# Reordering VectorE's work in the expert steps of a graph and mixture-of-experts kernel: result adds ahead of the second matrix' low part, and the last step's second matrix made ready earlier

## Chip, cores and metric

The kernel runs on one core of a Trainium2 chip. The metric is device time in microseconds; three runs of the kernel before have a median of 1210.55 us.

## What is computed

Two GraphSAGE layers and then a mixture of experts, all in float32, on 1250 rows of 1024 features. Only the expert part is touched:

```python
t = layernorm(x)                                   # [1250, 1024]
logits = silu(t @ rw1 + rb1) @ rw2 + rb2           # 8 experts
vals, idx = top_k(logits, 2); w = softmax over the two
eh = silu(einsum('td,edh->teh', t, ew1) + eb1)     # hidden 256
eo = einsum('teh,ehd->ted', eh, ew2) + eb2
y = t + einsum('te,ted->td', w, eo)
out = x + y
```

## The kernel before

The router sorts the 2 x 1250 (row, expert) pairs by expert into blocks, and 17 **expert steps** (NS) of 256 rows (M) go through them, each with one expert's two matrices: ew1 (1024 x 256, 1 MB) and ew2 (256 x 1024, 1 MB). Everything that is multiplied is split in two parts of reduced precision: a high part that ScalarE writes as a copy, and a low part, which is what VectorE gets by subtracting the high part from the raw value. Each product is then three matmuls (high x high, high x low, low x high). The step number is s; u is the buffer (s % 2), every tile has two; b counts the step's two halves of 128 rows.

Each engine has its own written order, and semaphores join them. `pipeline(e, n, (lag, part), ...)` (line 70) runs through t = 0, 1, ..., and in each t calls each part with s = t - lag, in the order of the list; `skewed` (line 86) is the pair (0, head), (1, tail).

- **SP** (lines 1892 to 1906) loads the raw matrices, w1 and w2 of step s, 1 MB each. Each load waits until VectorE has made the low part of step s - 2 of the same matrix (m_wlo, which is given 2 at the start), since the raw buffer is free then.
- **TensorE** (1939 to 1989), step t: the first product of step t in two halves of 24 matmuls (L1969), each followed by 8 transposes of the gathered rows of step t + 1 (L1955), then the second product of step t - 1, 4 groups of 6 matmuls (L1985), one for each 128 rows x 512 columns.
- **ScalarE** (1997 to 2043), step t: `shift(t - 1)` writes bias times router weight into o_rows (L2035), which waits for m_kept; then `head(t)`: SiLU of the first product (L2021), the high part of the transposed rows of step t + 1 (L2015), of the hidden values (L2026), of the first matrix of step t + 1 (`w1`, L2005), and of the second matrix of step t (`w2`, L2010).
- **VectorE** (2045 to 2083), step t: the low part of the transposed rows of step t + 1 (L2056, 4 groups), of the hidden values of step t (L2062), of the first matrix of step t + 1 and of the second matrix of step t (both L2051); then `tail(t - 1)`: 4 adds of the second product, times the router weight, into o_rows (L2073). The first two adds complete half b = 0, the other two b = 1; each raises m_out.
- **GpSimd** (1908 to 1937) issues the indirect DMAs. `scatter(s)` (L1921) adds the 256 finished rows of o_rows to `out` in memory, in two halves. As rows may repeat between steps, it first waits until both halves of the scatter of step s - 1 have landed (m_st); only then does it raise m_kept, which releases ScalarE's `shift(s + 1)`; each half then waits for its two adds. The gather of 256 rows (L1928), in two halves as well, reads the inputs of a later step.

Of the kernel before, what the change touches and what calls it, by code (L numbers as in the profile page):

```python
# [62 lines left out]
NS = (TOP * N + NX * (M - 1)) // M  # L63
# [6 lines left out]
def pipeline(e, n, *stages):  # L70


    deepest = max(lag for lag, _ in stages)
    for t in range(n + deepest):
        for lag, part in stages:
            if 0 <= t - lag < n:
                part(t - lag, (t - lag) % 2, (t - lag) // 2)
# [8 lines left out]
def skewed(e, n, head, tail):  # L86

    pipeline(e, n, (0, head), (1, tail))


def build(nc, I, out):
    ctx = ExitStack()
    with ctx:
        prog = {k: [] for k in ("sync", "scalar", "vector", "gpsimd", "tensor")}

        def on(engine):

            return prog[engine].append
# [216 lines left out]
        w2_raw = S("w2_raw", [128, 2, HK, D], F32)  # L315
        w2_hi = S("w2_hi", [128, 2, HK, D], F32R)
        w2_lo = S("w2_lo", [128, 2, HK, D], F32R)
# [27 lines left out]
        def wait_apart(e, sem, value):  # L345


            e.wait_ge(sem, value)
            e.sem_inc(s_none, 1)

        @on("gpsimd")
        def _(e):
            e.memset(zero[:], 0.0).then_inc(s_id, 1)
            e.memset(ident[:], 0.0).then_inc(s_id, 1)
            e.wait_ge(s_id, 2)
            e.affine_select(out=ident[:], in_=ident[:], compare_op=ALU.not_equal, fill=1.0, base=0,
                            pattern=[[-1, 128]], channel_multiplier=1).then_inc(s_id, 1)
            e.memset(ones[:], 1.0).then_inc(s_ones, 1)
            e.memset(epst[:], EPS).then_inc(s_ones, 1)
# [371 lines left out]
        def four(engine, table, s, top_):  # L731

            _, values = nc.values_load_multi_w_load_instructions(table[0:1, s:s + 4], engines=[engine], min_val=0, max_val=top_)
            return values
# [1150 lines left out]
        def gated(e):  # L1885

            e.wait_ge(g_x, 1)
            base_stored(e)
            for u in range(2):
                e.wait_ge(t_st[u], 32 * (NT // 2))  # L1890
# [100 lines left out]
        def more(s):  # L1991
            return not isinstance(s, int) or s < NS - 1
# [4 lines left out]
        @on("scalar")  # L1997
        def _(e):
            gated(e)
            e.wait_ge(g_eb, 32)  # L2000

            def w1(s, u, q):
                e.wait_ge(m_win[0][u], 16 * q + 16)
                e.wait_ge(m_g1, HK * s + HK)
                e.activation(w1_hi[:, u], w1_raw[:, u], ACT.Copy).then_inc(m_whi[0], 1)  # L2005

            def w2(s, u, q):
                e.wait_ge(m_win[1][u], 16 * q + 16)
                e.wait_ge(m_g2, NB * s + NB)
                e.activation(w2_hi[:, u], w2_raw[:, u], ACT.Copy).then_inc(m_whi[1], 1)  # L2010

            def rows(s, u, q, groups=range(4)):
                for g in groups:
                    e.wait_ge(m_tx, 4 * s + g + 1 + 8)
                    e.activation(group(xt_hi, u, g), bank(g), ACT.Copy).then_inc(m_xhi, 1)  # L2015

            def head(s, u, q):
                x = e.value_load(step_x[0:1, ds(s, 1)], min_val=0, max_val=NX - 1)
                for j in range(HK):
                    wait_apart(e, m_g1, HK * s + j + 1 + 4)  # L2020
                    e.activation(hid[:, u, j, :], ps[:, 2 + j, 0:M], ACT.Silu, bias=eb1c[:, ds(x * HK + j, 1)]).then_inc(m_h, 1)  # L2021
                    if more(s):
                        rows(s + 1, 1 - u, q + u, range(2 * j, 2 * j + 2))
                e.wait_ge(m_h, HK * s + HK + 2)
                e.wait_ge(m_g2, NB * s + NB)
                e.activation(hid_hi[:, u], hid[:, u], ACT.Copy).then_inc(m_hhi, 1)  # L2026
                if more(s):
                    w1(s + 1, 1 - u, q + u)
                w2(s, u, q)

            def shift(s, u, q):
                x = e.value_load(step_x[0:1, ds(s, 1)], min_val=0, max_val=NX - 1)
                e.wait_ge(m_kept, s + 1)
                for b in range(SUB):
                    e.activation(o_rows[:, u, b, :], eb2_all[:, ds(x, 1), :].rearrange("p a n -> p (a n)"), ACT.Copy,  # L2035
                                 scale=slot_w[:, ds(s * SUB + b, 1)]).then_inc(m_eb, 1)

            e.sem_inc(m_out, 2 * NB)
            w1(0, 0, 0)
            rows(0, 0, 0)  # L2040
            e.wait_ge(g_to, 2)
            e.wait_ge(g_b2, 16)
            pipeline(e, NS, (1, shift), (0, head))

        @on("vector")
        def _(e):
            gated(e)

            def w(i, raw, hi, lo, s, u, q):
                e.wait_ge(m_whi[i], s + 1)  # L2050
                e.tensor_tensor(lo[:, u], raw[:, u], hi[:, u].bitcast(F32), ALU.subtract).then_inc(m_wlo[i], 1)  # L2051

            def rows(s, u, q, groups=range(4)):
                for g in groups:
                    e.wait_ge(m_xhi, 4 * s + g + 1)
                    e.tensor_tensor(group(xt_lo, u, g), bank(g), group(xt_hi, u, g).bitcast(F32), ALU.subtract).then_inc(m_xlo, 1)  # L2056

            def head(s, u, q):
                if more(s):
                    rows(s + 1, 1 - u, q + u)  # L2060
                e.wait_ge(m_hhi, s + 1)
                e.tensor_tensor(hid_lo[:, u], hid[:, u], hid_hi[:, u].bitcast(F32), ALU.subtract).then_inc(m_hlo, 1)  # L2062
                if more(s):
                    w(0, w1_raw, w1_hi, w1_lo, s + 1, 1 - u, q + u)
                w(1, w2_raw, w2_hi, w2_lo, s, u, q)

            def tail(s, u, q):
                for b in range(SUB):
                    e.wait_ge(m_eb, SUB * s + b + 1)
                    for half in range(2):  # L2070
                        e.wait_ge(m_g2, NB * s + 2 * b + half + 1 + 2 * NB)
                        cols = o_rows[:, u, b, 512 * half:512 * half + 512]
                        e.scalar_tensor_tensor(out=cols, in0=ps[:, 4 + 2 * b + half, :], scalar=slot_w[:, ds(s * SUB + b, 1)],  # L2073
                                               in1=cols, op0=ALU.mult, op1=ALU.add).then_inc(m_out, 1)
            w(0, w1_raw, w1_hi, w1_lo, 0, 0, 0)
            rows(0, 0, 0)
            e.wait_ge(g_pe, 5)
            e.tensor_copy(parts3[:], ps[:, 6, 0:3 * NB_]).then_inc(g_sl, 1)
            e.wait_ge(g_sl, 1)
            e.tensor_tensor(slot_w[:], parts3[:, 2 * NB_:3 * NB_], parts3[:, NB_:2 * NB_], ALU.add).then_inc(g_sl, 1)  # L2080
            e.wait_ge(g_sl, 2)
            e.tensor_tensor(slot_w[:], slot_w[:], parts3[:, 0:NB_], ALU.add).then_inc(g_to, 1)
            skewed(e, NS, head, tail)


        @on("sync")
# [39 lines left out]
```

## Time and profile before

| what | value |
|---|---|
| median of 3 runs | 1210.55 us (1208.05 to 1214.05) |
| profiled execution, own time | 1209.29 us |
| its span, first to last instruction | 1207.6 us |
| TensorE busy | 1099.3 us, 91% of the span |
| VectorE busy | 641.2 us, 53% |
| ScalarE busy | 459.7 us, 38% |
| moved by DMA | 160.18 MB, mean 133 GB/s |
| the 17 expert steps | from about 940 us to the end |

The times of instructions below are microseconds from the start of the span. The matmul ends are modelled, and descriptors and transfers of a DMA are not part of the instruction that issues it: the row of a DMA_INDIRECT is the time in which GpSimd writes its descriptors. A wait is shown in brackets behind a row, as the idle time of the engine before it and what ended that.

### The profile page before, as it was taken

To read this page: it belongs to the slowest core of one execution; us is meant where nothing else is said; L and a number is where in the kernel's file an instruction comes from. 1 tells how busy PE (TensorE), PEld (TensorE's weight loads), DVE (VectorE), ACT (ScalarE), POOL (GpSimd) and SP (SyncE) were. 2 spreads that over 40 slices of the span, in tenths; PEclk is the share of its full clock that TensorE was granted. 3 is DMA by queue.
4 is the path that set the end of the run, shared out by engine and by line. 5 is a ranking of instruction groups with operands and counts; after the bars stand their busy time and mean duration, and the time that the engine had idled before them with its cause. 6 is when DMAs were issued, how large, how long until landed. Compare 5 with 4: busy or idle time off the path is not lost.

```text
span 1207.6 us, 19102 instructions
## 1 busy us (share of the span) xinstructions
PE 1099.3 (91%) x6584; PEld 1026.7 (85%) x6584; DVE 641.2 (53%) x1112; ACT 459.7 (38%) x939; POOL 158.5 (13%) x178
## 2 busy tenths in 40 slices
PE   2698999999998999999999999999994799999992
PEld 1697888888888999999999999999993698888882
DVE  5737777777836243225223522642225477777772
ACT  5643434343511222111112011552332566766770
POOL 2000000000000002000200200014421133333322
PEclk9999999999999999999999999999997699999997
DMA  5411331133123752014102400765541779999975
GB/s 132 130 38 62 100 94 51 56 100 100 45 85 102 225 159 58 1 28 141 46 1 102 136 1 1 221 201 157 182 179 60 288 248 309 294 300 297 307 178 90
DMA packets 74817, 160.18 MB, mean 133 GB/s; under 512 B 11135, under 2 KB 49980, under 8 KB 70226
## 3 DMA queue, kind: packets, MB, share of 16 engines
q1 hardware_dynamic: 61117, 112.34, 29.6%
q0 software_dynamic: 12992, 45.90, 14.7%
q8 instruction: 68, 1.11, 0.4%
q10 hardware_dynamic: 596, 0.48, 0.1%
q14 instruction: 44, 0.35, 0.1%
HBM read 112.07 MB, written 46.63 MB: 131 GB/s over the span
## 4 chain that ended last, share of the span: by engine, by line
PE 55%; DMA 5%; DVE 5%; issue 2%; ACT 2%; POOL 0%; ACTq 0%; SPq 0%; POOLq 0%; DVEq 0%; PEld 0%
PE ps L1366 19%; PE ps L1438 9%; PE ps L1405 7%; PE ps L1097 7%; PE ps L1969 5%; DMA out<-o_rows,to_i 4%; PE ps L1985 4%; DVE w_lo L2051 2%; PE ps L1955 2%; PE ps L854 1%; ACT w_hi L2005 1%; DVE o_rows L2073 1%; DMA self_part<-self_d 1%; PE ps L1424 1%; ACT o_rows L2035 1%
## 5 line engine op out<-in xcount | busy, mean ns | idle before, releaser
L729 DVE TENSOR_TENSOR adj<-ps,adj 125x250 f32 x212 | 87.7, 414 | 65.5 <-issue 30.6
L854 PE MATMUL ps<-h_lo,w_hi 128*128 128x418 f32 x336 | 109.2, 372 | 0.0
L1328 POOL TENSOR_TENSOR s_rows<-s_rows,b1t 125x1368 f32<-125x1368 f32 (+3 forms) x9 | 23.6, 2633 | 644.8 <-DMA s_rows<-in_x 644.8
L854 PE MATMUL ps<-h_hi,w_hi 128*128 128x418 f32 x336 | 100.4, 380 | 0.0
L722 PE MATMUL ps<-key_hot,src_hot 125*125 125x250 bf16 x424 | 81.9, 274 | 16.3 <-DVE adj L729 13.1
L1405 PE MATMUL ps<-z_hi,adj 125*125 125x342 f32 (+1 forms) x300 | 95.1, 322 | 1.3 <-DVE s_rows L1637 1.3
L1405 PE MATMUL ps<-z_lo,adj 125*125 125x342 f32 (+1 forms) x300 | 94.3, 319 | 1.4 <-issue 1.4
L854 PE MATMUL ps<-h_hi,w_lo 128*128 128x418 f32 x336 | 93.5, 359 | 0.0
L1097 PE MATMUL ps<-adj,y_hi 125*128 125x416 f32 (+1 forms) x240 | 85.6, 357 | 4.1 <-issue 3.4
L722 PEld LDWEIGHTS ps<-key_hot,src_hot 125*125 125x125 bf16 x424 | 51.8, 136 | 44.0 <-issue 22.6
L1969 PE MATMUL ps<-xt_hi,w_hi 128*128 128x256 f32 x272 | 81.9, 301 | 7.0 <-DVE w_lo L2051 5.5
L2051 DVE TENSOR_TENSOR w_lo<-w_raw,w_hi 128x2048 fp32r<-128x2048 f32 x34 | 76.5, 2289 | 20.2 <-ACT w_hi L2005 19.0
L1097 PE MATMUL ps<-adj,y_lo 125*128 125x416 f32 (+1 forms) x240 | 85.4, 356 | 0.4 <-issue 0.4
L1969 PE MATMUL ps<-xt_lo,w_hi 128*128 128x256 f32 x272 | 78.7, 289 | 0.0
L1969 PE MATMUL ps<-xt_hi,w_lo 128*128 128x256 f32 x272 | 78.6, 289 | 0.0
L1366 PE MATMUL ps<-wn_hi,hs_lo 128*125 128x342 f32 (+1 forms) x240 | 76.7, 320 | 0.0
L1366 PE MATMUL ps<-wn_hi,hs_hi 128*125 128x342 f32 (+1 forms) x240 | 76.7, 320 | 0.0
L1366 PE MATMUL ps<-ws_hi,hs_hi 128*125 128x342 f32 (+1 forms) x240 | 76.7, 320 | 0.0
L1366 PE MATMUL ps<-ws_lo,hs_hi 128*125 128x342 f32 (+1 forms) x240 | 76.7, 319 | 0.0
L1366 PE MATMUL ps<-ws_hi,hs_lo 128*125 128x342 f32 (+1 forms) x240 | 76.6, 319 | 0.0
L1366 PE MATMUL ps<-wn_lo,hs_hi 128*125 128x342 f32 (+1 forms) x240 | 76.5, 319 | 0.0
L704 ACT ACTIVATE src_now<-scol 125x4 f16 x212 | 41.3, 195 | 92.0 <-DVE key_hot L715 76.7
(282 smaller groups left out, 2767.9 us busy)
## 6 DMA issues: line engine op xcount, KB each, us to landing
w_raw<-in_L_ffn_ew SPq DMA_DIRECT2D x34, 1024.0 KB
xin<-in_x SPq DMA_DIRECT2D x10, 448.0 KB
t_d<-xn SPq DMA_DIRECT2D x10, 448.0 KB
base<-x_d POOLq DMA_DIRECT2D x10, 448.0 KB, 4.2
out<-base POOLq DMA_DIRECT2D x10, 448.0 KB, 3.5
y_d<-y_hi SPq DMA_DIRECT2D x7, 625.0 KB
y_d<-y_lo SPq DMA_DIRECT2D x7, 625.0 KB
self_d<-self SPq DMA_DIRECT2D x7, 625.0 KB
```

The costliest lines, as they stand in the source:

```text
L704: e.activation(src_now[:, b, :, :], twice(scol), ACT.Copy)
L722: mm = e.matmul(ps[0:P, 5 + b % 2, 0:KW], src_hot[:, b, g, 0:P], key_hot[:, b, g, :], start=(g == 0), stop=(g == G - 1))
L729: e.tensor_tensor(cols, ps[0:P, 5 + b % 2, 0:KW].rearrange("p (t w) -> p t w", t=NT), cols, ALU.add).then_inc(self.took, 1)
L854: mm = e.matmul(BANK(m, own, c), wt[:, own, k, :], ht[:, k, a:a + w], start=(k == 0 and p == 0), stop=(k == KT - 1 and p == 2))
L1097: mm = e.matmul(ps[:, banks[c], 0:w], y[:, k, :], adj_[:, k, a:a + w], start=(n == 1), stop=(n == 2 * NT))
L1366: mm = e.matmul(ps[0:P, 2 * v + u, 0:w], ht[:, u, k, :], wt[v][:, k, 0:w], start=(k == EARLY[0] and p == 0), stop=(k == LATE_K[-1] and p = ...
L1405: mm = e.matmul(ps[0:P, 2 + n % 2, 0:w], adj_[:, k, tile_of(j)], z[:, k, 0:w], start=(k == 0 and p == 0), stop=(k == NT - 1 and p == 1))
L1438: mm = e.matmul(ps[:, i % 5, 0:w], wt[u][:, k, :], ht[:, k, a:a + w], start=(n == 1), stop=(n == 3 * KT))
L1955: mm = e.transpose(ps[:, g % 2, k * M + 128 * b:k * M + 128 * b + 128], x_rows[:, u, b, 128 * (2 * g + k):128 * (2 * g + k + 1)], ident[:])
L1969: mm = e.matmul(ps[:, 2 + j, 0:M], wt[:, u, k, 128 * j:128 * j + 128], xt[:, u, k, :], start=(n == 1), stop=(n == 3 * KT))
L1985: mm = e.matmul(ps[:, 4 + 2 * b + half, :], ht[:, u, j, 128 * b:128 * b + 128], wt[:, u, j, 512 * half:512 * half + 512], start=(n == 1), ...
L2051: e.tensor_tensor(lo[:, u], raw[:, u], hi[:, u].bitcast(F32), ALU.subtract).then_inc(m_wlo[i], 1)
```

## The change

VectorE's step keeps the same instructions in another order: the 4 adds of step t - 1 come ahead of the low part of the second matrix of step t. In the last step the low part of the second matrix is made first of all, ahead of the hidden values' low part. ScalarE writes the last step's high part of the second matrix at the start of that step, ahead of `shift` and `head`, rather than at its end.

```diff
@@ -2026,9 +2026,11 @@
                 e.activation(hid_hi[:, u], hid[:, u], ACT.Copy).then_inc(m_hhi, 1)
                 if more(s):
                     w1(s + 1, 1 - u, q + u)
-                w2(s, u, q)
+                    w2(s, u, q)
 
             def shift(s, u, q):
+                if s == NS - 2:
+                    w2(s + 1, 1 - u, q + u)
                 x = e.value_load(step_x[0:1, ds(s, 1)], min_val=0, max_val=NX - 1)
                 e.wait_ge(m_kept, s + 1)
                 for b in range(SUB):
@@ -2058,11 +2060,16 @@
             def head(s, u, q):
                 if more(s):
                     rows(s + 1, 1 - u, q + u)
+                else:
+                    w(1, w2_raw, w2_hi, w2_lo, s, u, q)
                 e.wait_ge(m_hhi, s + 1)
                 e.tensor_tensor(hid_lo[:, u], hid[:, u], hid_hi[:, u].bitcast(F32), ALU.subtract).then_inc(m_hlo, 1)
                 if more(s):
                     w(0, w1_raw, w1_hi, w1_lo, s + 1, 1 - u, q + u)
-                w(1, w2_raw, w2_hi, w2_lo, s, u, q)
+
+            def second(s, u, q):
+                if more(s):
+                    w(1, w2_raw, w2_hi, w2_lo, s, u, q)
 
             def tail(s, u, q):
                 for b in range(SUB):
@@ -2080,7 +2087,7 @@
             e.tensor_tensor(slot_w[:], parts3[:, 2 * NB_:3 * NB_], parts3[:, NB_:2 * NB_], ALU.add).then_inc(g_sl, 1)
             e.wait_ge(g_sl, 2)
             e.tensor_tensor(slot_w[:], slot_w[:], parts3[:, 0:NB_], ALU.add).then_inc(g_to, 1)
-            skewed(e, NS, head, tail)
+            pipeline(e, NS, (0, head), (1, tail), (0, second))
 
 
         @on("sync")
```

## Rows read from the trace of the kernel before

**Rows 1.** Windows before and with scatters: PE, PEld, DVE, ACT, POOL, PEclk, DMA, GB/s.
```profile
971.00:984.00 13.00, 13.00 (x89) 11.72 (x88) 9.96 (x12) 8.85 (x12) 5.03 (x4) 1.00 0.63 219
...
1060.00:1080.00 20.00, 19.15 (x134) 17.16 (x133) 13.83 (x18) 14.04 (x19) 8.33 (x6) 1.00 1.02 327
```

**Rows 2.** Waits, 960 to 1208 us: total, times, longest.
```profile
ACT o_rows L2035 <- POOLq L1918: 57.3, 15, 5.3
```

**Rows 3.** VectorE timeline: start, length, instruction, idle before.
```profile
973.22 4.49 DVE L2051 TENSOR_TENSOR w_lo<-w_raw,w_hi 128x2048 fp32r<-128x2048 f32 x2 [0.93 <-ACT w_hi L2005]
...
1054.92 4.50 DVE L2051 TENSOR_TENSOR w_lo<-w_raw,w_hi 128x2048 fp32r<-128x2048 f32 x2 [1.04 <-ACT w_hi L2005]
1059.33 2.72 DVE L2073 SCALAR_TENSOR_TENSOR o_rows<-ps,slot_w,o_rows 128x512 f32<-128x512 f32 x4
...
1069.08 4.49 DVE L2051 TENSOR_TENSOR w_lo<-w_raw,w_hi 128x2048 fp32r<-128x2048 f32 x2 [1.03 <-ACT w_hi L2005]
...
1082.74 4.49 DVE L2051 TENSOR_TENSOR w_lo<-w_raw,w_hi 128x2048 fp32r<-128x2048 f32 x2 [1.03 <-ACT w_hi L2005]
...
1097.87 4.50 DVE L2051 TENSOR_TENSOR w_lo<-w_raw,w_hi 128x2048 fp32r<-128x2048 f32 x2 [1.04 <-ACT w_hi L2005]
...
1111.12 4.49 DVE L2051 TENSOR_TENSOR w_lo<-w_raw,w_hi 128x2048 fp32r<-128x2048 f32 x2 [0.93 <-ACT w_hi L2005]
```

**Rows 4.** ScalarE timeline: preparing the output rows.
```profile
991.83 2.19 ACT L2035 ACTIVATE o_rows<-eb_all,slot_w 128x1024 f32 x2 [3.60 <-POOLq L1918]
...
1061.02 2.19 ACT L2035 ACTIVATE o_rows<-eb_all,slot_w 128x1024 f32 x2 [4.33 <-POOLq L1918]
...
1074.67 2.19 ACT L2035 ACTIVATE o_rows<-eb_all,slot_w 128x1024 f32 x2 [3.81 <-POOLq L1918]
...
1089.81 2.19 ACT L2035 ACTIVATE o_rows<-eb_all,slot_w 128x1024 f32 x2 [5.30 <-POOLq L1918]
...
1102.89 2.19 ACT L2035 ACTIVATE o_rows<-eb_all,slot_w 128x1024 f32 x2 [3.25 <-POOLq L1918]
...
1157.92 2.19 ACT L2035 ACTIVATE o_rows<-eb_all,slot_w 128x1024 f32 x2 [3.66 <-POOLq L1918]
```

**Rows 5.** GpSimd timeline: issues of the scatter's first half.
```profile
979.92 1.65 POOL L1921 DMA_INDIRECT out<-o_rows,to_i  x1 [6.81 <-DVE o_rows L2073]
...
1061.78 1.61 POOL L1921 DMA_INDIRECT out<-o_rows,to_i  x1 [6.74 <-DVE o_rows L2073]
...
1145.49 1.61 POOL L1921 DMA_INDIRECT out<-o_rows,to_i  x1 [6.54 <-DVE o_rows L2073]
```

**Rows 6.** DMA queues, 1008.2 to 1011.9 us: packets, MB, share of 16 engines.
```profile
q1 hardware_dynamic: 186, 1.40, 97.5%
q0 software_dynamic: 9, 0.03, 2.8%
```

**Rows 7.** VectorE timeline, the end.
```profile
1165.98 4.49 DVE L2051 TENSOR_TENSOR w_lo<-w_raw,w_hi 128x2048 fp32r<-128x2048 f32 x2 [1.03 <-ACT w_hi L2005]
1170.39 2.72 DVE L2073 SCALAR_TENSOR_TENSOR o_rows<-ps,slot_w,o_rows 128x512 f32<-128x512 f32 x4
...
1177.53 2.29 DVE L2051 TENSOR_TENSOR w_lo<-w_raw,w_hi 128x2048 fp32r<-128x2048 f32 x1 [1.11 <-ACT w_hi L2010]
1179.74 2.72 DVE L2073 SCALAR_TENSOR_TENSOR o_rows<-ps,slot_w,o_rows 128x512 f32<-128x512 f32 x4
```

**Rows 8.** GpSimd timeline, the end.
```profile
1172.59 1.56 POOL L1921 DMA_INDIRECT out<-o_rows,to_i  x1 [10.06 <-DVE o_rows L2073]
...
1183.00 1.58 POOL L1921 DMA_INDIRECT out<-o_rows,to_i  x1 [6.99 <-DVE o_rows L2073]
...
1192.62 1.56 POOL L1921 DMA_INDIRECT out<-o_rows,to_i  x1 [6.17 <-DMA out<-o_rows,to_i]
```

**Rows 9.** ScalarE timeline, the end.
```profile
1175.59 1.90 ACT L2010 ACTIVATE w_hi<-w_raw 128x2048 fp32r<-128x2048 f32 x1
1181.85 2.20 ACT L2035 ACTIVATE o_rows<-eb_all,slot_w 128x1024 f32 x2 [4.35 <-POOLq L1918]
```

## The prediction

> **What bounds the kernel now.** Only the 17 expert steps change, so I read views of that stage alone. First the windows [rows 1]: with scatters running, TensorE is busy 19.15 of 20 us at full granted clock, VectorE 13.83, ScalarE 14.04, and the DMA engines are occupied all the time (share 1.02, 327 GB/s), against 0.63 before scatters begin. TensorE is the engine to fill; the DMA share is the warning. Next the waits [rows 2]: the largest that a busy engine has is ScalarE's, 57.3 us in 15 waits for GpSimd's line 1918. That line releases `shift` once the scatter before has landed. ScalarE works in order, so SiLU and the high part of the next rows are queued behind `shift`, VectorE's low part behind these, and TensorE's transposes behind that. A late landing thus becomes a gap on TensorE.
>
> How late is too late stands in the timelines. Let W be the start of a step's pair of w_lo subtractions (the beat), O the start of `shift` in the next beat. From W to the next W [rows 3], with O - W [rows 4]:
> - O 5.02 after 1097.87: next beat in 13.25 us
> - 5.59 after 1069.08: 13.66
> - 6.10 after 1054.92: 14.16
> - 7.07 after 1082.74: 15.13
>
> That is a line: step = 13.25 + (O - W - 5.18), and never under 13.25. So 13.25 us is what TensorE needs by itself. From the W at 973.22 to the one at 1165.98 [rows 3, 7] are 14 steps in 192.76 us, 13.77 each; 14 x 13.25 is 185.5. **The late landings cost 7.3 us.**
>
> Why is O late? The adds start 4.41 after W, behind both subtractions (1059.33 against 1054.92) [rows 3]. The scatter is issued once two adds are done and the previous one has landed: where adds decide, 6.6 after W (1172.59 - 1165.98) [rows 7, 8]; where the landing decides, 0.76 after O (1061.78 against 1061.02) [rows 4, 5]. From the first half's issue to O (the latency D) is 11.91 us for the first (979.92 to 991.83) and 12.43 for the 13th (1145.49 to 1157.92) [rows 4, 5]; the 13 between them average 12.71. The loop closes: O comes 6.6 + 12.7 = 19.3 after the W before it, hence 19.3 - step after its own, and step = 13.25 + 19.3 - step - 5.18 gives 13.7, close to the 13.77 seen.
>
> **The change, part by part.**
>
> *Adds ahead of the second subtraction, steps 1 to 15.* Nothing is added or removed; the 4 adds start 2.2 us earlier (half the pair of 4.49), the second subtraction 2.72 later, the length of the adds [rows 3]. Their inputs are there: `shift` for them ran in the previous beat, and TensorE's last group of the second product ends near the start of the second subtraction, so at most the fourth add waits, a fraction of its 0.7 us. Adds-gated issues now stand 4.4 after W. With D unchanged, O is 17.1 after W, 3.9 after the next: 1.3 inside the 5.18. The other gate now bites: scatters can't follow each other in under D + 0.76 = 13.47 us. O drifts 0.22 us a step against 13.25, uses up the 1.3 in 6 steps, and the 7 or so left cost 0.22 each, 1.6 us. D is not even, and long ones can't be won back by short ones: the average loop gives 13.71 where 13.77 came out, so I take another 0.7 us over the steps. Gain: 7.3 - 1.6 - 0.7 = **5.0 us**.
>
> D is the one unknown. Nothing in the trace shows a scatter asked for ahead of the weights. Before, SP asks for the two raw matrices at the end of the pair, 2.2 us ahead of the first half's issue, and while they move the scatter's queue gets 2.8% of the engines against 97.5% [rows 6]. Afterwards that request comes at W + 7.1 (4.41 + 2.72), 2.7 behind the first half's issue and just behind the second's, as the first takes GpSimd 1.6 [rows 5]. Lower bound: no weights in the way, 9.26 (1172.59 to 1181.85) [rows 8, 9]; then all 7.3 us are won. Upper bound: the whole pair cuts in between the halves, 2 MB at the 1.40 MB in 3.7 us of [rows 6], 5.4 us more: 14.7. I keep 12.7, the nearest rows, which are of the same loaded stage; below it the result hardly moves.
>
> For two requests at once the Trainium skill (DMA: Bandwidth & Descriptors, Queues, rings and completion order) says that each DMA engine takes turns between queues, packet by packet. By that rule the weights would slow the second half but not hold it, and D would lie between my bounds; rows 6 show no such turns within that stretch.
>
> *What the later subtraction delays.* TensorE needs the second matrix of step t only in the next beat, some 9 us on. SP queues nothing but loads behind that wait; w2 of step t + 2 and w1 of step t + 3 are asked for 2.7 later, with a beat and a half until ScalarE copies them: 0 us. Were that cover gone, each late load would cost what it is late. VectorE's next rows wait for ScalarE in any case: 0.
>
> *Last step.* ScalarE's copy of the second matrix, 1.9 us [rows 9], moves ahead of `shift(15)`. It waits for its load and for TensorE to be done with step 14; SiLU of the first half slips by about 1 us and is still ready before the second half's end, which hid_lo needs: 0. On VectorE, the 2.29 us subtraction (1177.53) leaves the place between hid_lo and the adds [rows 7] for one in which VectorE waited. Without this part TensorE's last product would wait for a subtraction behind adds that wait for TensorE.
>
> *The end.* Scatters decide here, each waiting for the one before: issues at 1172.59, 1183.00, 1192.62 [rows 8]; the middle one follows the landing (1181.85) [rows 9], not its adds (from 1179.74) [rows 7]. The first was adds-gated and now comes 2.2 us earlier, and the two behind it follow: **2.2 us**, on top of the steps'.
>
> Sum: 5.0 + 2.2 = 7.2 us off the profiled 1209.29, 1202.1. The median of the runs stands 1.26 us higher, so 1203.3 for the median.
>
> **Rivals.**
> 1. *The DMA engines are the bound.* Share 1.02 [rows 1]: if each step's 4 MB fill the engines for its 13.77 us, an earlier scatter only pushes weights and gathers back, and D shrinks for none. Only the end gains: 1210.6 - 2.2 = 1208.4. For: no idle window once scatters run. Against: single steps took 13.25 at the same load, and weights have slack to be late in. The Trainium skill (Perfetto Trace Analysis, Identifying the Most-Contended Engine) says to judge DMA by bandwidth against the memory's peak, since occupancy misleads; by that rule this rival loses weight, by the share alone it keeps it.
> 2. *No stalls left.* D falls towards 9.26: 7.3 + 2.2 = 9.5 off, 1201.1. For: the first half now starts before the weights. Against: the second half does not.
> 3. *The weights cut the scatter in two (slower).* The pair lands between the halves and D rises. The point is D = 13.0: above it D + 0.76 exceeds 13.77 and scatter after scatter paces the kernel. At D = 14.0, 14.76 a step, 1.0 x 14 = 14 us more, less 2.2: 1222. For: [rows 6], weights once begun hold the queue. Against: the first half is under way 2.7 us sooner, and the weights must wait for it in turn.
> 4. *The edit does nothing to D or to the gate that decides*: landings gate everything already. 1210.6. Against: 1172.59 and the 6.6 us loop are adds-gated.
>
> **How the numbers follow.** About 0.5% (6 us) is what a measurement of this kernel can tell from no change, so 1204.5 is the line. Chances: forecast 0.53, of which some 0.1 falls short of the line; rival 1 0.22; rival 2 0.16; rival 3 0.07; rival 4 0.02. Faster 0.53 - 0.1 + 0.16 = 0.59; slower 0.07 and a little for an unseen late load, 0.08; same 0.33. The range runs from rival 2 less the runs' own scatter of about 1.5 (1199.5) to rival 1 plus 2 (1210.5), leaving out the slower case. The likeliest case's own range is 1201 to 1206.
>
> **What would show it.** Right: ScalarE's wait for line 1918 falls from 57.3 to some 30 us; adds start 2.2 after W; mean step 13.3 to 13.5; O - W near 4 at first, creeping up; D at 9.3 to 12.7; the last three scatters shift by the step gain plus 2.2. Wrong: O - W stays above 5.2, D rises by what the scatter is earlier (rival 1), D over 13 (rival 3), or new waits of w_hi for its load.

## The result, and the profile after

| | us |
|---|---|
| predicted | 1203.3 (1199.5 to 1210.5) |
| after, median of 4 runs | 1224.35 (1222.33 to 1227.4) |
| before, median of 4 runs | 1209.3 (1207.81 to 1214.05) |
| ratio, 95% interval | 1.0119 (1.0086 to 1.0153) |
| profiled execution after, own time (span) | 1224.77 (1223.0) |

The change makes the kernel 1.2% slower, outside the range. The profiled executions are 15.5 us apart, and the loss is where the gain was looked for. From the start of the w_lo pair at 975.61 to that at 1181.45 the same 14 steps take 205.84 us, 14.70 each, where they took 192.76 [rows 3, 7]: 13.1 us more instead of 5.0 less. The end, from hid_lo of step 15 to the issue of the last scatter, takes 29.33 us where it took 28.36: 1.0 more instead of 2.2 less. The remaining 1.4 us lie outside these two stretches, where nothing was edited.

Windows of the kernel after, columns as in [rows 1]; the third and fourth are one microsecond each:

```profile
1060.00:1080.00 20.00, 18.18 (x106) 15.56 (x104) 13.21 (x15) 13.92 (x17) 7.12 (x6) 0.91 1.00 292
...
976.00:1191.00 215.00, 200.32 (x1295) 177.71 (x1294) 153.16 (x161) 135.74 (x161) 74.04 (x54) 0.98 0.91 264
...
1043.00:1044.00 1.00, 0.00 (x0) 0.00 (x0) 0.04 (x1) 1.00 (x4) 0.70 (x2) 1.00 1.23 410
...
1046.00:1047.00 1.00, 1.00 (x4) 0.87 (x4) 0.69 (x1) 0.55 (x2) 0.00 (x0) 0.50 0.99 295
```

TensorE is idle for 14.7 us of these 215. The DMA engines are as occupied as in [rows 1], and move less (292 against 327 GB/s): a share of 1.00 is not a sign that they are used to the full. The waits of 960 to 1224 us, as in [rows 2]:

```profile
POOL out L1921 <- DMA out<-o_rows,to_i: 90.3, 12, 10.7
ACT o_rows L2037 <- POOLq L1918: 70.5, 15, 6.7
...
PE ps L1955 <- DVE xt_lo L2058: 14.7, 11, 2.6
```

ScalarE's wait was to fall from 57.3 to some 30 us and has risen to 70.5. The first row says why: GpSimd now waits 12 times for the landing of the scatter before, and not for the adds as in [rows 5]. The third row is TensorE's transposes, starved at the far end of that chain. The timelines of GpSimd and, below, of ScalarE:

```profile
980.11 1.65 POOL L1921 DMA_INDIRECT out<-o_rows,to_i  x1 [4.60 <-DVE o_rows L2080]
982.06 2.14 POOL L1921 DMA_INDIRECT out<-o_rows,to_i  x1 [0.30 <-issue]
...
1010.31 1.61 POOL L1921 DMA_INDIRECT out<-o_rows,to_i  x1 [7.46 <-DMA out<-o_rows,to_i]
...
1025.53 1.61 POOL L1921 DMA_INDIRECT out<-o_rows,to_i  x1 [7.81 <-DMA out<-o_rows,to_i]
...
1055.53 2.48 POOL L1921 DMA_INDIRECT out<-o_rows,to_i  x1 [6.00 <-DMA out<-o_rows,to_i]
...
1187.04 2.97 POOL L1921 DMA_INDIRECT out<-o_rows,to_i  x1 [9.36 <-DVE o_rows L2080]
1190.32 1.90 POOL L1921 DMA_INDIRECT out<-o_rows,to_i  x1 [0.31 <-issue]
```

```profile
994.68 2.19 ACT L2037 ACTIVATE o_rows<-eb_all,slot_w 128x1024 f32 x2 [4.04 <-POOLq L1918]
1009.55 2.19 ACT L2037 ACTIVATE o_rows<-eb_all,slot_w 128x1024 f32 x2 [5.04 <-POOLq L1918]
1024.78 2.19 ACT L2037 ACTIVATE o_rows<-eb_all,slot_w 128x1024 f32 x2 [5.39 <-POOLq L1918]
```

D is 980.11 to 994.68 = **14.57 us** at the first scatter (11.91 before) and 14.14 in the mean of the first 13 (12.71). Each scatter follows O at the 0.76 us of the prediction (1010.31 - 1009.55, 1025.53 - 1024.78), and this gap of 0.75 or 0.76 stands in 11 of the first 12. The chain of waits of the kernel after, from 1000 us on, has no VectorE in it:

```profile
1010.31 1.61 POOL out L1921
1011.92 0.30 issue
1012.22 12.40 DMA out<-o_rows,to_i
1024.62 0.03 POOLq L1918
...
1025.53 1.61 POOL out L1921
```

So the kernel runs at the pace of the scatters: D + 0.76 = 14.90, near the 14.70 seen. VectorE does what the edit says (timeline, after):

```profile
1017.61 2.29 DVE L2053 TENSOR_TENSOR w_lo<-w_raw,w_hi 128x2048 fp32r<-128x2048 f32 x1 [1.04 <-ACT w_hi L2005]
1019.82 2.72 DVE L2080 SCALAR_TENSOR_TENSOR o_rows<-ps,slot_w,o_rows 128x512 f32<-128x512 f32 x4
1022.46 2.27 DVE L2053 TENSOR_TENSOR w_lo<-w_raw,w_hi 128x2048 fp32r<-128x2048 f32 x1
...
1032.84 2.29 DVE L2053 TENSOR_TENSOR w_lo<-w_raw,w_hi 128x2048 fp32r<-128x2048 f32 x1 [1.04 <-ACT w_hi L2005]
```

The adds come 2.2 us after W. Here O - W is 1024.78 - 1017.61 = 7.17, the line of the prediction gives 15.24 and the step took 15.23.

Why has D grown? SP's requests for the weights, after:

```profile
982.76 2.33 SPq L1905 DMA_DIRECT2D w_raw<-in_L_ffn_ew  x2
...
1009.89 1.44 SPq L1905 DMA_DIRECT2D w_raw<-in_L_ffn_ew  x2
```

and before:

```profile
1004.41 1.42 SPq L1905 DMA_DIRECT2D w_raw<-in_L_ffn_ew  x2
```

Before, the request stood 2.36 us ahead of the first half's issue (at 1006.77). At the first scatter after, it stands 2.65 behind the first half's issue and 0.70 behind the second's, and what the DMA queues do is seen in three stretches (983 to 985, 986 to 988, 989 to 993 us; q0 carries scatters and gathers, q1 weights; packets, MB, share of 16 engines):

```profile
q0 software_dynamic: 83, 0.34, 96.8%
...
q1 hardware_dynamic: 75, 0.61, 99.5%
...
q0 software_dynamic: 107, 0.44, 55.3%
q1 hardware_dynamic: 105, 0.74, 46.9%
```

The first half moves first (from 982 to 986 the queue q0 carries 0.52 MB, which is 128 rows of 4 KB), then the weights alone, then the scatter's second half and the weights take turns. The second half, on which the landing hangs, thus waits for part of the weights and shares the engines with the rest.

That is the picture of the first scatter only. Later the scatters have slipped, and the request stands near the first half's issue again: at 1009.89 it is 0.42 ahead, and over the first 13 scatters it lies between 2.65 behind and 2.00 ahead, 0.1 ahead in the mean. The weights then go first: at the fourth one (request 1024.76, 0.77 ahead of the issue at 1025.53) only they move from 1027 to 1031, nearly as in [rows 6], and from 1031 to 1034 the two queues share the engines (q1 56.4%, q0 43.9%). D is 15.36 there, and 12.78 at the fifth, whose request is 2.00 ahead as before. The less is left of the 2.2 us of lead, the more of the weights still stands in front of the scatter or beside it; between these two D scatters, and not every value of it was traced.

### The profile page after: what moved, and what is told of

Read it like the earlier page. It is cut to its first block, busy times and chain, and to the rows that moved or that the text cites. A ratio compares the mean times of both kernels' runs of the same rounds, so it can differ in the third digit from the quotient of the medians.

```text
span 1223.0 us, 19102 instructions
## 1 busy us (share of the span) xinstructions
PE 1105.2 (90%) x6584; PEld 1032.3 (84%) x6584; DVE 638.0 (52%) x1112; ACT 458.9 (38%) x939; POOL 163.3 (13%) x178
## 4 chain that ended last, share of the span: by engine, by line
PE 49%; DMA 14%; issue 3%; POOL 2%; DVE 2%; ACT 1%; POOLq 0%; DVEq 0%; ACTq 0%; PEld 0%
PE ps L1366 18%; DMA out<-o_rows,to_i 14%; PE ps L1438 9%; PE ps L1405 8%; PE ps L1097 8%; POOL out L1921 2%; PE ps L854 1%; PE ps L1969 1%; PE ps L1424 1%; PE ps L822 0%; PE ps L1955 0%; DVE w_lo L2053 0%; PE ps L1447 0%; PE ps L1449 0%; PE ps L1985 0%
## 5 line engine op out<-in xcount | busy, mean ns | idle before, releaser
L2058 DVE TENSOR_TENSOR xt_lo<-ps,xt_hi 128x512 fp32r<-128x512 f32 x68 | 44.0, 686 | 64.0 <-ACT xt_hi L2015 64.0
```

## Experiments

D (from the issue of a scatter's first half to O, the start of the `shift` that its landing releases) is the mean of the first 13 scatters, "step" that of the 14 steps from hid_lo of step 1 to hid_lo of step 15, "end" the time from there to the issue of the last scatter's first half, all of one profiled execution; the ratio is to the kernel before, timed beside it. Before: D 12.71, step 13.76, end 28.36. After: 14.14, 14.69, 29.33.

| kernel | median, us | ratio (95%) | D | step | end |
|---|---|---|---|---|---|
| e1 | 1226.60 | 1.0120 (1.0087 to 1.0153) | 14.13 | 14.66 | 28.73 |
| e2 | 1226.98 | 1.0112 (1.0080 to 1.0143) | 14.24 | 14.92 | 28.77 |
| e3 | 1221.55 | 1.0092 (1.0060 to 1.0124) | 14.18 | 14.76 | 26.78 |
| e4 | 1210.19 | 0.9984 (0.9969 to 1.0000) | 12.62 | 13.70 | 28.52 |
| e5 | 1222.64 | 1.0091 (1.0062 to 1.0120) | 12.58 | 14.87 | 26.36 |
| e6 | 1222.00 | 1.0104 (1.0069 to 1.0140) | 10.87 | 14.52 | 28.64 |
| e7 | 1203.89 | 0.9936 (0.9915 to 0.9958) | 10.90 | 13.27 | 28.12 |
| e8 | 1209.28 | 0.9989 (0.9966 to 1.0011) | 12.85 | 13.50 | 31.12 |
| e9 | 1216.14 | 1.0030 (1.0011 to 1.0049) | 13.63 | 14.43 | 28.46 |
| e10 | 1198.69 | 0.9902 (0.9877 to 0.9926) | 11.05 | 13.28 | 28.12 |
| e11 | 1207.08 | 0.9979 (0.9959 to 0.9999) | 12.79 | 13.81 | 28.05 |
| e12 | 1199.56 | 0.9923 (0.9900 to 0.9946) | 10.77 | 13.25 | 25.68 |

### e1 and e2: the request for the weights behind the scatter's issue

The same edit on the kernel after (e1) and on the one before (e2): from step 3 on, SP asks for the second matrix (and so for the first one queued behind it) only once GpSimd has passed both halves' issues.

```diff
@@ SP, load of step s, w = 1 is the second matrix
                     e.wait_ge(m_wlo[w], s + 1)
+                    if w == 1 and s >= 3:
+                        e.wait_ge(m_sent, s - 2)
                     e.dma_start(raw[:, u], ...)
@@ GpSimd, scatter, after the loop over halves
+                e.sem_inc(m_sent, 1)
```

> The changed kernel, and SP asks for the second matrix of step s (and so for what is queued behind it) only once GpSimd has issued both halves of the scatter of step s - 3. Theory A (the weights, asked for in the middle of the scatter's issue, cut it in two, D rises to 14.1 us, and scatter after scatter paces the kernel at D + 0.76): D falls to 9.3 to 10.5 us, a step takes 13.25, no stalls for late landings; 9 us under before, about 1200. Theory B (the DMA engines are full, order does not matter): 13.8 us a step or more, 1207 to 1225. Theory C (VectorE's second subtraction slows GpSimd's writing of descriptors, 2.0 to 3.0 us instead of 1.6 in 4 issues): that overlap stays, so the time stays near 1224.

> The kernel before with the same added wait on SP and nothing else. Theory A: the scatter, still issued 6.6 us after W, has the queues to itself; D 9.5 to 10.5, O - W about 3, 13.25 a step, so 7 us under before, about 1202. Theory B: no gain, 1209 or a little slower. Theory C: no gain, 1209, since GpSimd's issues were not slowed there.

e1 changed nothing that can be told from the kernel after (its ratio and D are the same): the request comes 0.52 to 0.88 behind the first issue in 12 of the 13 scatters, where it was 0.1 ahead in the mean. Theory A's fall of D did not come, since both runs put the request behind the first issue's start and not behind its end. e2 is the run that decides. It has the VectorE order of before, and the loss is all there: 1.0112, D 14.24, steps of 14.92 = nearly D + 0.76. No wait of ScalarE for a late load stands in it, so it is not the weights' lateness that costs. Its SP and GpSimd rows show the request only 0.64 us behind the start of the first half's issue, so GpSimd's semaphore rose while that issue was still running. e2, SP timeline:

```profile
1060.71 1.43 SPq L1908 DMA_DIRECT2D w_raw<-in_L_ffn_ew  x2
```

e2, GpSimd timeline:

```profile
1060.07 1.61 POOL L1924 DMA_INDIRECT out<-o_rows,to_i  x1 [7.13 <-DVE o_rows L2077]
```

e2, DMA queues from 1066 to 1069 us, columns as above:

```profile
q0 software_dynamic: 77, 0.32, 53.8%
q1 hardware_dynamic: 74, 0.61, 50.3%
```

The two share the engines about evenly. A request 3 us later relative to the scatter than before thus costs the 1.5 us of D and the whole of the loss, with no change on VectorE.

### e3 and e4: each part of the change alone

e3 is the kernel after without the last step's part:

```diff
@@ ScalarE, head and shift
-                    w2(s, u, q)
+                w2(s, u, q)
...
-                if s == NS - 2:
-                    w2(s + 1, 1 - u, q + u)
@@ VectorE, head and second
-                else:
-                    w(1, w2_raw, w2_hi, w2_lo, s, u, q)
...
-                if more(s):
-                    w(1, w2_raw, w2_hi, w2_lo, s, u, q)
+                w(1, w2_raw, w2_hi, w2_lo, s, u, q)
```

e4 is the kernel after with the adds behind the second subtraction again:

```diff
-            pipeline(e, NS, (0, head), (1, tail), (0, second))
+            pipeline(e, NS, (0, head), (0, second), (1, tail))
```

> Adds ahead of the second subtraction in all steps, but the last step's second matrix made ready late, as before. Theory A: all of the slowdown is there, since it comes from steps 1 to 15: 1224 to 1228, the end some 0 to 3 us longer than in the changed kernel. A rival, that the last step's moved copy causes the loss, gives 1209 or less.

> The last step's second matrix made ready early as in the changed kernel, the order of all other steps as before. Theory A: steps as before (13.77 us, D 12.7), the end 0 to 1 us shorter as its first scatter is still issued 6.6 after W: 1208 to 1209.5. The rival that this part is at fault gives 1220 or more.

The steps' loss belongs to the adds' place alone (e3: 14.76 a step; e4: 13.70). The last step's part by itself is worth about nothing (0.9984, its interval touches 1). But the parts don't add up, and not as expected (the end 0 to 3 us longer in e3): with the adds early, the last step's part lengthens the end from 26.78 to 29.33 us. The GpSimd rows of the kernel after at 1187.04 and 1190.32 show how: the two issues take 2.97 and 1.90 us instead of 1.56, and lie under this row of its VectorE timeline, the second matrices of steps 15 and 16 back to back:

```profile
1186.30 4.48 DVE L2053 TENSOR_TENSOR w_lo<-w_raw,w_hi 128x2048 fp32r<-128x2048 f32 x2
```

The last section comes back to it.

### e5 and e6: no weights while a scatter moves

SP's wait is for the landing of the last scatter under way, on the kernel after (e5) and before (e6):

```diff
                     e.wait_ge(m_wlo[w], s + 1)
+                    if w == 1 and s >= 3:
+                        for b in range(SUB):
+                            e.wait_ge(m_st[1 - u][b], 16 * ((s - 3) // 2 + 1))
                     e.dma_start(raw[:, u], ...)
```

> Two runs told SP to ask for the weights once the scatter was issued, but GpSimd's sequencer raises a semaphore while the issue still runs: the request came 0.6 us behind the start of the first half's issue, so weights still ran beside the scatter, and D stayed at 14.1 to 14.2. Here, in the changed kernel, SP asks only once both halves of the scatter of step s - 3 have landed. Theory A (what counts is how much of the weights runs beside the scatter): D falls to 9.3 to 10.5, a step to 13.25 to 13.6, 5 to 9 us under before. Theory B (the DMA engines are full, order only moves who waits): the weights are then late, ScalarE waits for them, and the time is at or above before's.

> The kernel before with the same wait of SP for the landed scatter. Theory A: D 9.5 to 11, O - W under 5.18, steps of 13.25 to 13.6, 3 to 7 us under before; the end as in before. Theory B: at or above before, with waits of ScalarE for the weights.

Without weights beside it D is 10.87 in e6, as theory A had it, so some 1.8 us of before's 12.71 were the weights' doing. But these now come too late, as theory B had it, and the time is no better. e6, waits from 960 to 1228 us:

```profile
PE ps L1972 <- DVE w_lo L2054: 22.0, 12, 5.5
...
ACT w_hi L2008 <- DMA w_raw<-in_L_ffn_ew: 15.2, 10, 3.2
```

5.5 us of TensorE's 22.0 are one wait near the start that every kernel here has; the rest is new, and so is ScalarE's wait for the load. The loss is the same 1%, by another mechanism. In e5 D is 12.58, though the weights are out of the way there too. There D is no longer the scatter's latency alone: its steps are bound by late weights (ScalarE waits 16.9 us for w_raw), and ScalarE waits for the landing ahead of `shift` in only 5 of the 13 cases, with D at 11.2 to 12.5; in the others it comes late itself, with D up to 14.96. The issues of the second halves are also 0.6 us longer (see e8 and e9).

### e7: the first matrix asked for ahead of the second

If weights behind a scatter hurt and weights after its landing come too late, they should go earlier. Before, SP queues w1 of step t + 3 behind w2 of step t + 2, and so asks for both at the end of the subtraction pair. Swapped, w1 can leave when its own buffer is free, 2.2 us sooner:

```diff
-            pipeline(e, NS, (0, head))
+            load(0, 0, 0)
+            load(1, 0, 0)
+            load(0, 1, 1)
+            for s in range(1, NS):
+                if s < NS - 1:
+                    load(0, s + 1, 1 - s % 2)
+                load(1, s, s % 2)
```

(load(w, s, u) is the body of SP's old head for one matrix; VectorE and ScalarE are those of before.)

> The kernel before, SP's queue alone reordered: the first matrix of step s + 1 is asked for ahead of the second of step s, so one of the two megabytes is asked for 2.2 us earlier (4.4 ahead of the scatter's issue, the other 2.2 as before). Theory A: less of the weights is left when the scatter's packets come, D 11 to 12.2, 2 to 5 us under before. Theory B: no change, within 2 us.

**0.9936 (0.9915 to 0.9958).** 12 of the 14 steps take 13.24 or 13.25 us, the floor of the prediction. e7, windows:

```profile
1060.00:1080.00 20.00, 19.98 (x144) 18.45 (x144) 16.60 (x19) 12.64 (x16) 7.07 (x6) 1.00 1.02 340
```

e7, waits from 960 to 1210 us:

```profile
ACT o_rows L2041 <- POOLq L1924: 38.5, 15, 4.3
```

e7, SP timeline:

```profile
1060.34 0.34 SPq L1905 DMA_DIRECT2D w_raw<-in_L_ffn_ew  x1
...
1062.55 0.34 SPq L1905 DMA_DIRECT2D w_raw<-in_L_ffn_ew  x1
```

e7, GpSimd timeline:

```profile
1064.53 1.61 POOL L1927 DMA_INDIRECT out<-o_rows,to_i  x1 [6.69 <-DVE o_rows L2079]
```

The request for the first matrix is 4.19 us ahead of the scatter's issue, that for the second 1.98. D is 10.90, a little under the 11 to 12.2 expected, and TensorE is busy 19.98 of 20 us with a DMA share of 1.02. That refutes rival 1: the same bytes at the same share go through at 340 GB/s, with no stall. The steps shrink by 14 x (13.76 - 13.27) = 6.9 us, and the medians are 6.7 apart: this is the 7.3 us that the prediction found, won by another edit.

### e8 and e9: does the request order mend the kernel after?

e8 is the kernel after with one matrix' load cut from 128 to 16 partitions from step 3 on, so that a step moves 0.9 MB less:

```diff
-                    e.dma_start(raw[:, u], view[ds(x, 1)]...)
+                    rows = slice(0, 16 if w == 0 and s >= 3 else 128)
+                    e.dma_start(raw[rows, u], view[ds(x, 1), rows]...)
```

e9 is the kernel after with e7's SP order.

> The changed kernel, but from step 3 on only 16 of the 128 partitions of the first matrix are loaded, the others keep an old expert's values: 0.9 of 2 MB of weights a step less. Theory A: D falls by about half of what the weights add to the unloaded 9.3, to 11 to 12, and steps to 13.25: about 1200. If the slowdown had another cause than weights beside the scatter (VectorE's order, GpSimd's issue), D stays over 13.5 and the time near 1224.

> The changed kernel with SP's queue reordered as in the run before that took steps of 13.25 us (first matrix of step s + 1 asked for ahead of the second of step s). One megabyte is asked for at W + 2.2, 2.2 us ahead of the scatter's issue at W + 4.4, the other at W + 7.1, in the middle of it. Theory A: only the second one cuts in: D 12 to 13, O - W about 4 to 5, steps 13.25 to 13.7, 4 to 9 us under before. If VectorE's order itself is what costs, it stays above 1218.

Less data brings D from 14.14 to 12.85 and the step to 13.50, so the weights weigh on D, though less than expected (11 to 12, and about 1200 us). The new order helps much less than in e7: e9 loses 0.3% where e7 gains 0.6% and 4 to 9 us were expected. Its second matrix is still asked for behind the late subtraction. And in both kernels GpSimd's issues have grown. e9, GpSimd timeline:

```profile
1077.39 3.22 POOL L1927 DMA_INDIRECT out<-o_rows,to_i  x1 [5.43 <-DVE o_rows L2086]
```

e9, VectorE timeline:

```profile
1076.84 2.28 DVE L2059 TENSOR_TENSOR w_lo<-w_raw,w_hi 128x2048 fp32r<-128x2048 f32 x1
```

The subtraction has 2.28 - (1077.39 - 1076.84) = 1.73 us left when the issue starts, and the issue takes 1.6 more than its 1.61. In e9 12 issues are longer so, by 12.9 us together, in e8 14 by some 14.2; spread over the first 13 scatters that is 0.8 us of D in each, about what both miss of their expected D. e8's end of 31.12 us holds an issue of 4.54. In the kernel after, the issues come so late that few of them meet a subtraction (3.9 us in all, 1.8 of them at the end).

### e10, e11 and e12: what beats both kernels

e11 leaves the steps as they were before and puts the adds first in step NS - 2 alone, with the change's last-step part:

```diff
-            pipeline(e, NS, (0, head), (0, second), (1, tail))
+            for t in range(NS + 1):
+                u, q = t % 2, t // 2
+                if t < NS:
+                    head(t, u, q)
+                    if t < NS - 2:
+                        second(t, u, q)
+                if t > 0:
+                    tail(t - 1, 1 - u, (t - 1) // 2)
+                if t == NS - 2:
+                    second(t, u, q)
```

e10 is e11 with e7's SP order. e12 is e10 without the last-step part: its second matrix stays behind the adds in both last steps (`if NS - 2 <= t < NS` in the last condition, ScalarE as before).

> SP's reordered queue on the kernel before, and the change's two edits kept only from step 15 on, where no load waits for the delayed subtraction any more. Theory A: steps 13.25 as without the end's edits, and the first of the last three scatters issued 2.2 us earlier with the others behind it: 2 us under the 1203.9 of the run without them, 8 to 9.5 under before.

> The kernel before with the change's two edits kept only from step 15 on. It measures the prediction's term for the end by itself: the scatter of step 14 issued 4.4 us after W instead of 6.6, all steps before it unchanged: 2.2 us under before. A rival, that a late landing gates that scatter anyway, gives 0 to 1.

> SP's reordered queue on the kernel before, and from step 15 on the adds ahead of the second subtraction, but without the last step's early second matrix. In the traces so far an issue of a scatter that starts while a w_lo subtraction runs on VectorE takes longer by what is left of that subtraction (1.6 us becomes 1.8 to 3.7); with both subtractions of the last steps back to back behind the adds it took 4.49 us (the run with the end's edits), which ate the 2.2 us won. Theory: here the second half's issue meets one subtraction alone and takes 2.3 us; from the last hid_lo but one to the last scatter's second issue it is some 26.8 us as in the run of the first part alone, not 28.1; the steps 13.25. So 1 to 1.5 us under the run with both edits, 9 to 12 under before. If TensorE's late last product decides the end instead, it is equal or slower than that run.

(In the last text 26.8 is e3's time to the *first* issue of the last scatter; to the second, which the text names, e3 takes 28.64 and e12 27.54. To the first e12 takes 25.68.)

e11 measures the prediction's term for the end by itself. Its ratio is 0.9979 (0.9959 to 0.9999), 0.1 to 5 us, which holds the 2.2 us expected but can't tell it from the rival's 0 to 1. The profile of one execution shows less: the end is 28.05 us against 28.36, 0.3 shorter, with the same lengthened issue as in e10, below.

e10 at 0.9902 and e12 at 0.9923 beat both kernels, and their intervals overlap. e10's stage is no shorter than e7's in the profiles (185.85 + 28.12 against 185.82 + 28.12 us); it started 7.7 us earlier, from work ahead of it that no edit touches. So its lead over e7 isn't shown to be its edit's, and its median is 13.0 us below before's where its steps and end are 7.0 shorter. The intervals of e12 and e7 overlap too, and e12, expected 1 to 1.5 us under e10, is not: its shorter end, below, is seen in its profile alone. At the end e10 gains nothing, since the issue of the scatter's second half stands under the subtraction pair. e10, GpSimd timeline:

```profile
1161.08 1.56 POOL L1927 DMA_INDIRECT out<-o_rows,to_i  x1 [8.07 <-DVE o_rows L2086]
1162.94 4.49 POOL L1927 DMA_INDIRECT out<-o_rows,to_i  x1 [0.30 <-issue]
```

e10, VectorE timeline:

```profile
1161.52 4.48 DVE L2059 TENSOR_TENSOR w_lo<-w_raw,w_hi 128x2048 fp32r<-128x2048 f32 x2
```

The first issue came 2.2 us earlier against hid_lo (6.12 us behind it, 8.33 before), and the second was lengthened by 2.9. With one subtraction there instead of two, e12 has 2.29 us at the same place and an end 2.4 us shorter. e12, GpSimd timeline:

```profile
1166.64 2.29 POOL L1927 DMA_INDIRECT out<-o_rows,to_i  x1 [0.31 <-issue]
```

## Why the prediction was wrong

**D kept at 12.7 "the nearest rows": the step that failed.** The prediction had seen that the request for the weights moves from 2.2 us ahead of the first half's issue to 2.7 behind it, had both bounds (9.26 and 14.7), and then took a value measured with the request ahead. The nearest row was near in stage, not in the thing that the edit changes. Measured: 14.57 at the first scatter, where the request is 2.65 behind, and 14.14 in the mean, though the request comes back to 0.1 ahead of the issue as the scatters slip: near the upper end all the same. e2 shows that this order alone does it. The steps' term, 5.0 us of gain, became 13.1 us of loss by it.

**Rival 3's "against" failed with it.** Its price was nearly right (1222 for D = 14.0, measured 1224.35 for 14.14), as was its point of decision, D = 13.0. Part of that nearness is luck: at D = 14.14 its rule gives 14 x (14.90 - 13.77) = 15.8 us for the steps, which took 13.1 more, and the 2.2 us that it took off for the end did not come. It was given 0.07 because "the first half is under way 2.7 us sooner, and the weights must wait for it in turn". They do wait, for the first half (q0 at 96.8% in 983 to 985 us), but the landing that counts is the second half's. For that one the weights go first (q1 at 99.5%), and then take every other turn. And later in the stage the weights are hardly behind any more and move ahead of both halves (1027 to 1031), so that the scatter cut in two is traced for the first one alone. On two requests at once the prediction cited the Trainium skill (DMA: Bandwidth & Descriptors, Queues, rings and completion order). Where both queues have been moving for a while, the traces agree (53.8% and 50.3%); in the first two or three microseconds after one of them starts they do not, here as in [rows 6].

**The gain in the steps, 5.0 us,** had the right source. The loop, the floor of 13.25 us, the line step = 13.25 + (O - W - 5.18) and the gate at O + 0.76 all hold after: of the 14 steps, 12 lie within 0.02 us of the line. That the landing gate would bite was foreseen; with D at 14.1 it is the pace of the whole stage. (The average loop, 13.25 + 19.3 - 5.18 halved, is 13.69 and not 13.71, which would have made the 0.7 us some 1.1.)

**The last 2.2 us** were half right: the issue moves as said, but what the earlier issue itself meets was left out. The first issue does come 2.2 us earlier against hid_lo where it is adds-gated (e3 6.11, e10 6.12), and e3's end is 1.6 us shorter, e12's 2.7. In the kernel after it was lost: the scatter before landed late (the issue is 7.31 behind hid_lo), and both issues were lengthened. In e11, with before's steps, the second issue is 2.9 us longer, and 0.3 us of the gain are left.

**The last step's part, costed at 0,** is about 0 alone (e4), and costs 2.5 us beside early adds (e3 against after). The prediction moved the subtraction from its place to "one in which VectorE waited", and didn't ask what GpSimd did meanwhile.

**Weights asked for 2.7 us later: 0 us.** No wait of w_hi for its load appears after, so that cover held. It has little left over: waiting for the landing uses it up (e5, e6).

**Rival 1,** the likeliest of the rivals at 0.22, is refuted by e7. **Rival 2** had about the right size of what could be won (9.5 us; in the profiles e12's steps and end together are 9.8 us shorter than before's, and its median is 8.9 below the kernel before), but not for this edit. The scatter's latency falls when the weights go well ahead of it, not when the scatter goes ahead of them.

## What to carry to other kernels

When an edit moves an instruction, list the requests that its semaphore releases and put them on the same time line as the transfers of other queues: the order in which two queues are asked can be worth more than the instruction's own place. A term whose nearest row was measured in the other order must not be taken from that row. And look at what runs on GpSimd under each two-input VectorE instruction that you move.

## What the runs showed of the hardware

- **A scatter's issue waits for a VectorE subtraction under way.** Each indirect scatter issue that starts while a w_lo subtraction (two SBUF inputs) runs is longer by about what is left of it: 2.48 us at 1055.53 (after; 1.61 otherwise), 3.22 in e9. Under a back-to-back pair it is 4.49 in e10, the rest of both, but 2.97 at 1187.04 (after), the rest of the first alone; what decides between these was not tested. In before, e2, e6 and e7, where none starts under one, none is longer. One issue that came first (980.11, after) did not hold up the subtraction that started 0.35 later, and took its usual 1.65. The Trainium skill (SBUF — State Buffer, Who interferes with whom) states that a VectorE instruction with two SBUF inputs contends with a GpSimd instruction that reads SBUF, and that the order of issue decides which of the two blocks; the prediction overlooked it. The traces agree where the subtraction came first; the issue at 980.11 blocked nothing. The same section infers that this form doesn't hold up the writing of descriptors; for these issues the runs show that it does.
- **A queue that starts late gets next to nothing at first.** In after, with scatter packets under way at 96.8% (983 to 985 us), the weights' first packets came 2.2 to 2.5 us after their request at 982.76; in before, with idle engines, 1.0 to 1.3 after the one at 977.74. They then had 99.5% while the scatter's second half, whose issue had begun 0.70 us before they were asked for, stood still; then came turns of 55.3% and 46.9%. In before the first scatter, issued at 979.92 behind the weights, had its first packet only at 985.0, when they were nearly through. Why the turns begin late was not tested.
- **GpSimd's semaphore instruction overtakes the issue before it.** In e1 and e2 SP's request, which waits for "both halves issued", started 0.52 to 0.88 us after the first issue had begun (12 of the first 13 scatters of each), though each issue takes 1.6.
- **TensorE's granted clock fell after two of the stalls.** After 2.6 idle us at 1042 to 1044.7, the window 1046 to 1047 stands at 0.50, the 1.2 GHz level, and the clock is back at 1.00 by 1049. The two steps around it are 0.43 and 0.86 us over the line of the prediction, the only ones that leave it: 1.3 of the 13.1 us. A second fall, to 0.50 from 1077 to 1079 after 1.8 idle us, is what the 0.91 of the window 1060 to 1080 shows; its steps stay on the line. e2 has four falls. Over the same 14 steps before and e7 were granted 1.00.
